# Two of every 125 row gathers of a graph kernel moved from GpSimd's indirect DMA to ScalarE, one transfer per row

## The reference

```python
def _L2_gnn_ref(feat, weight, src, dst, etypes):
    num_rels = weight.shape[0]                         # 16
    h_src = feat[src]
    msg = jnp.zeros((h_src.shape[0], weight.shape[2]), dtype=feat.dtype)
    for r in range(num_rels):
        mask = etypes == r
        msg = msg + h_src * mask[:, None].astype(feat.dtype) @ weight[r]
    return jax.ops.segment_sum(msg, dst, num_segments=feat.shape[0])

x = _layernorm(x + _L0_gnn_ref(...), axis=-1)
x = _layernorm(x + _L1_gnn_ref(...), axis=-1)
x = _layernorm(x + _L2_gnn_ref(x, L2_gnn_weight, src, dst, edge_type_16), axis=-1)
x = _layernorm(x + _L3_gnn_ref(...), axis=-1)
```

## Time and profile before

| | us |
|---|---|
| median of three runs | 13239.03 |
| the profiled execution's own time | 13241.2 |
| its span, first to last instruction | 13239.5 |
| POOL busy | 9829.3 (74%) |
| DVE busy | 6151.1 (46%) |
| PE busy | 2706.8 (20%) |
| ACT busy | 1294.2 (10%) |
| 3125 gathers of the relational layer: POOL busy, and idle just before them | 2965.0 and 1015.6 |
| the loop over these gathers | 4881.6 to 8801.9 |

### The profile page before, as it was taken

The page is one execution under the profiler, slowest core; times in us unless marked ns, Lnnn a source line. Parts: engine busy times, 40 slices in busy tenths (PEclk is TensorE's granted clock), DMA queues, the critical chain, the costliest instruction groups (busy, mean ns, idle before and its releaser), DMA issues. The chain is left out here.

```text
span 13239.5 us, 78693 instructions
## 1 busy us (share of the span) xinstructions
PE 2706.8 (20%) x12129; PEld 1928.6 (15%) x12156; DVE 6151.1 (46%) x21235; ACT 1294.2 (10%) x3683; POOL 9829.3 (74%) x10101
## 2 busy tenths in 40 slices
PE   2000001111100360000000000013444444444445
PEld 2000001111100230000000000002222322223232
DVE  8666547777753442222222222223555555555554
ACT  3011101111111230000000000000100001010101
POOL 7777757777777767777777777777777777777774
PEclk6555555555555675555555555555666666666665
DMA  6333334444444342222222222222222222222221
GB/s 168 101 101 102 102 98 118 118 118 118 117 118 117 115 144 63 67 63 67 67 63 67 63 67 63 67 54 51 65 65 67 66 66 65 65 65 65 66 66 32
DMA packets 731548, 1103.23 MB, mean 83 GB/s; under 512 B 240731, under 2 KB 347192, under 8 KB 730567
## 3 DMA queue, kind: packets, MB, share of 16 engines
q0 software_dynamic: 332944, 306.83, 12.5%
q1 hardware_dynamic: 231478, 567.25, 11.4%
q10 hardware_dynamic: 167040, 228.30, 5.7%
HBM read 548.64 MB, written 552.93 MB: 83 GB/s over the span
## 5 line engine op out<-in xcount | busy, mean ns | idle before, releaser
L130 POOL DMA_INDIRECT g<-in_edge_attr,idxs x3072 | 3119.5, 1015 | 1018.4 <-issue 856.8
L130 POOL DMA_INDIRECT msg<-Y,idx x3125 | 2965.0, 949 | 1015.6 <-issue 952.1
L130 POOL DMA_INDIRECT yg<-ytab,idx x3125 | 2949.8, 944 | 962.8 <-issue 950.2
L1420 DVE SCALAR_TENSOR_TENSOR run<-run,same,msg 128x64 f32<-128x64 f32 x3125 | 890.9, 285 | 3029.8 <-DMA msg<-Y,idx 2922.3
L485 DVE SCALAR_TENSOR_TENSOR run<-run,sameD 128x80 f32<-128x80 f32 x3072 | 911.6, 297 | 1578.3 <-DMA g<-in_edge_attr,idxs 1038.5
L1814 DVE SCALAR_TENSOR_TENSOR run<-run,same,ps 128x32 f32<-128x32 f32 x3125 | 775.0, 248 | 1636.0 <-PE ps L1708 1533.0
L1008 PE MATMUL ps<-tail,before 128*128 128x64 f32 (+2 forms) x10 | 2.8, 421 | 4575.7 <-PEq L1322 3930.5
L489 DVE SCALAR_TENSOR_TENSOR runS<-runS,sameS,g 128x64 f32<-128x64 f32 x3072 | 856.4, 279 | 0.3
L1797 DVE SCALAR_TENSOR_TENSOR zx<-zx,same,zs 128x32 f32<-128x32 f32 x3124 | 792.3, 254 | 136.5 <-DVE anew L1780 29.1
L1689 PE MATMUL ps<-eaT,W1e 128*128 128x512 f32 (+1 forms) x394 | 401.1, 1121 | 1972.2 <-DMA yg<-ytab,idx 1971.6
L1816 DVE SCALAR_TENSOR_TENSOR run<-run,anew,ps 128x32 f32<-128x32 f32 x3125 | 758.4, 243 | 0.0
(11 more groups left out here) (325 smaller groups left out, 6042.2 us busy)
## 6 DMA issues: line engine op xcount, KB each, us to landing
R<-run SPq DMA_DIRECT2D x390, 320.0 KB, 2.3
R<-run SPq DMA_DIRECT2D x195, 512.0 KB, 2.7
R<-run SPq DMA_DIRECT2D x124, 800.0 KB, 3.8
v<-in_edge_attr ACTq DMA_DIRECT2D x384, 256.0 KB
RA<-runS SPq DMA_DIRECT2D x256, 256.0 KB, 3.0
Y<-tab SPq DMA_DIRECT2D x98, 512.0 KB
msg<-Y,idx POOLq DMA_INDIRECT x3125, 2.4
Z<-zeros SPq DMA_DIRECT2D x125, 400.0 KB, 4.2
```

Source lines behind the costliest of these rows:

```text
L130: eng.indirect_dma_start(out=out, out_offset=None, in_=table, in_offset=bass.IndirectOffsetOnAxis(ap=index, axis=0)).then_inc(sem, 16)
L1420: ins_ = v.scalar_tensor_tensor(out=run[:, q, t, :], in0=prev, scalar=same[:, q, t:t + 1], in1=msg[:, q, t, :], op0=ALU.mult, op1=ALU.add)
```

## The change

One tile in slot 1 and one in slot 3 of each chunk, tile 12 of the 25 (`BY_ROW`, `ROW_AT`), is no longer fetched by POOL. ACT fetches it. For that, SP writes the row numbers of these tiles once to a DRAM table `rows2` [50, 128], ahead of the load of `x` in `edges_01`. In `edges_2` ACT, behind its two copies for slot 1 or 3, loads 16 row numbers at a time into registers and issues one DMA of one row for each: 8 register loads and 128 DMAs to a tile. They raise the new semaphore `by_row[q]`, for which DVE waits as well as for `got[q]`.

```diff
+BY_ROW, ROW_AT, ROW_REGS = (1, 3), 12, 16
 ...
             sp.wait_ge(x_clear, 1)
+            for h, q in enumerate(BY_ROW):
+                sp.dma_start(k.rows2[h * CHUNKS2:(h + 1) * CHUNKS2, :].rearrange("c p -> p c"),
+                             k.rel_i[:, :].rearrange("p (c t) -> p c t", t=CH2)[:, :, SL2 * q + ROW_AT],
+                             allow_slow_non_contiguous=True).then_inc(settled, 16)
             sp.dma_start(k.X[0:LASTP, :, :], ins["x"][0:LASTP * NB, :].rearrange("(p b) f -> p b f", b=NB)).then_inc(settled, 16)
 ...
-            sp.wait_ge(settled, 16 * (NW + 5 + 2 + 6))
+            sp.wait_ge(settled, 16 * (NW + 5 + 4 + 6))
 ...
+        by_row = {q: sem(f"msg_rows{q}") for q in BY_ROW}
 ...
                     act.copy(same[:, q], k.same[:, at]).then_inc(meta_ready, 1)
+                    if q in by_row:
+                        fetch_rows(c, q)
+
+            def fetch_rows(c, q):
+                at = BY_ROW.index(q) * CHUNKS2 + c
+                for a in range(0, P, ROW_REGS):
+                    _, rows = nc.values_load_multi_w_load_instructions(
+                        k.rows2[bass.ds(at, 1), a:a + ROW_REGS], engines=[act.engine], min_val=0, max_val=NP * RELS - 1,
+                        skip_runtime_bounds_check_because="a source node and a relation give a row of Y")
+                    for i, row in enumerate(rows):
+                        act.dma_start(msg[a + i:a + i + 1, q, ROW_AT, :], k.Y[bass.ds(row, 1), :]).then_inc(by_row[q], 16)
 ...
                 for t in range(SL2):
+                    if q in by_row and t == ROW_AT:
+                        continue
                     gather(pool, msg[:, q, t, :], k.Y, idx[:, q, t:t + 1],
 ...
-                            v.wait_ge(got[q], 16 * SL2 * (c + 1))
+                            v.wait_ge(got[q], 16 * (SL2 - (q in by_row)) * (c + 1))
+                            if q in by_row:
+                                v.wait_ge(by_row[q], 16 * P * (c + 1))
```

More of the change, by code:

```diff
@@ L2110, in build @@
         k.Y = dram("Y", [NP * RELS, D])
+        k.rows2 = dram("rows2", [CHUNKS2 * len(BY_ROW), P], I32)
         k.ytab, k.ztab, k.Z = dram("ytab", [NP, MSG]), dram("ztab", [NP, MSG]), dram("Z", [E + NP, MSG])
```

## The result

The changed kernel takes 13,425.6 us (median of 4 runs, 13,401 to 13,455), the kernel before 13,239.7 beside it: ratio 1.0141, interval 1.0115 to 1.0166, so +186 us where +661 was forecast. The profiled execution's own time is 13,454.9 with a span of 13,452.5, 213.0 us over the span of before.

The account below looks back on a forecast made before the run. POOL's gathers bound the loop before; ACT's stream, 129.3 + 51.2 + 2 = 182.5 us a chunk, would bound it after. The loop's +651.5 and the setup's 9 make +660.5, so 13,900 us, range 13,190 to 14,450.

Parts of the forecast that it names:

- What bounds the loop: In the loop: POOL's stream of gathers alone, 1.2536 us a tile; 50 gathers removed are worth 62.7 us.
- ACT becomes the bound, POOL waits for its `same` copy: In the loop: ACT needs 182.5 us a chunk against POOL's 154.2, so POOL waits 28 us at slots 2 and 4.
- A group of loads, 3.2 us: In ACT's stream: table address, then 16 row numbers, two memory trips of 1.6 us; 51.2 us a chunk.
- An issue, 0.505 us: In ACT's stream: one transfer with its register computation, 256 a chunk, 129.3 us.
- the lower bound of 0.435: In ACT's stream: lowest price in us of a one-row transfer, 0.27 for the issue plus 0.165 for the rest.
- the loop's +651.5: The loop's forecast growth in us, 4571.9 instead of 3920.4.
- The range: Whole kernel: 13,190 to 14,450 us; the main forecast's own part, 13,275 to 14,450, varies loads from 1.6 to 4.5 us a group.
- Rival 1: In the loop: ACT keeps up if a load group costs at most 1.43 us; time about 13,205 us; chance 0.29.
- The setup, 9 us forecast: Ahead of the load of x: writing 6400 single numbers delays POOL one for one, 5.2 to 21 us, taken as 9.
- the upper bound, 53 ns for each single number of 4 bytes: In the setup: price from 640 numbers landing after 3.7 us, 40 to an engine; gives 21 us in all.
- Rivals 2 and 3: Rival 2: one-row issues wait for landings, 20,900 us, chance 0.04; Rival 3: setup cost eats the gain, about 13,239 us, 0.05.
- Rival 3: In the setup: ACT keeps up, but 6400 single numbers cost 36 us or more; time near 13,239 us; chance 0.05.

Follow-up runs that it names:

- e15: The changed kernel with one register load of 16 row numbers a tile instead of eight, all 6400 one-row transfers kept, output partly wrong: 13,213.0 us, ratio 0.9976.
- e12: The changed kernel with 32 row numbers to a register load instead of 16: 13,214.1 us, 0.9986 of the kernel before.
- e14: The kernel before plus only the setup, two loads of row numbers ahead of x, no tile fetched by ACT: 13,265.9 us, ratio 1.0027.
- e16: The changed kernel with only one tile of 125 fetched by ACT, that of slot 3: 13,227.5 us, 0.9974 of the kernel before.
- e13: The kernel before, no tile by row, with the load of x cut into 112 and 15 partitions: 13,162.3 us, ratio 0.9941.
- e2: The changed kernel with the row numbers loaded behind x, on a slow chip where the kernel before takes 15,850 us: ratio 1.1663.
- e5: The changed kernel with the row numbers loaded behind x, on a slow chip where the kernel before takes 15,790 us: ratio 1.178.
- e11: The changed kernel with the row numbers loaded behind x instead of ahead of it: 13,376.8 us, 1.0101 of the kernel before.

## Why the forecast was right in kind and wrong in size

1. **What bounds the loop: right.** POOL's stream was all of it; e15, which takes 50 gathers away and adds no wait, has the loop 65 us shorter than before against 62.7 forecast.
2. **ACT becomes the bound, POOL waits for its `same` copy: right**, but at slot 4 alone, not at 2 and 4, outside chunk 0. ACT's wait for DVE is gone, as foretold, and nothing else is late for it: the loop ends 3.4 us after POOL's last gather, 3.3 before, and the program 4437 us after the loop in both.
3. **A group of loads, 3.2 us: right, in part by luck.** 3.34 measured. The picture was two trips of 1.6 us; it is 1.15 for the address and 1.95 for 16 numbers, two misses that go opposite ways, and that second part grows by 0.108 a register (e12). The Trainium skill, "Runtime: NRT & Kernel Launch", section Instruction fetch mechanics, gives about 200 ns a register; the 18 registers of a group here took 3.1 us, 172 ns each, but the added registers only 108.
4. **An issue, 0.505 us: the step that failed.** It is 0.414 in the mean, 0.380 in the median, under the lower bound of 0.435 too. I took the step from transfers of 128 rows, whose DMA instruction takes 0.35; for one row it takes 0.224, less than any short-row issue of SP that the trace showed. The rest of a step is what it was there, 0.51 - 0.35 = 0.16 against 0.380 - 0.224. 256 x 0.091 = 23.3 us a chunk, 25 times over, is 582 us of loop; loads, copies and the loop's end took 4.3 a chunk more than forecast, 108 us, and the difference, 474, answers to the 472 by which the loop's +651.5 was too much (+179.4). The range held the time all the same, but by its width in another term: it let the loads run from 1.6 to 4.5 us a group and kept the issue at 0.505.
5. **The sum with measured terms closes.** 182.5 - 23.3 + 16 x 0.14 for the loads + 2.1 for the copies and the loop's end = 163.5 us a chunk. Counted another way, a tile takes 79.8 us in the mean from its first load to its last issue, and 4.0 us of a chunk are left for the rest. In the trace chunk 0 ends its last wait 141.8 us after the first gather, and chunks 1 to 24 take 163.5 us each (162.5 to 166.5). 141.8 + 24 x 163.5 + 34.4 behind the last wait = 4100.2; measured 4099.8.
6. **Why the error counted so much.** POOL has 154.2 us a chunk of its own, so only what ACT needs beyond that is paid: 28 us forecast, 9 measured. An error of 12% in ACT's chunk made the loss three times too large. The point from which Rival 1 decides was worked out from the same dear issue: at 0.414 an issue and 4 us of copies, a group may cost (154.2 - 106 - 4) / 16 = 2.76 us, and the real one missed that by 0.6. e12 gets below it, by its 5.0 us for 32 numbers, and comes out near Rival 1's 13,205 (13,214). Its waits in chunk 0 sum to 15 us, between the 23 and the 5 that Rival 1 names, but at slots 2 and 4, where Rival 1 has slot 4 alone, and its setup is dearer.
7. **The setup, 9 us forecast, 21 at the upper bound: 20 to 23 on POOL's stall, +21 by e14's span.** The row I kept as the upper bound, 53 ns for each single number of 4 bytes, came out right in its sum; going by the stores of the earlier trace rows, 13 ns a piece of 128 bytes, misled. Why a piece of 4 bytes costs more than one of 128 is not shown; the records of the single numbers in the changed kernel's trace have a median of 9 ns and a mean of 46, so a minority of long ones makes the price. e16, with half of the numbers, has half of the price: 9.9 us.
8. **Rivals 2 and 3 fell.** The longest of 6400 issues took 1.01 us, under the 1.6 of a landing, and the median 0.224, so issues do not wait for landings. Rival 3 needs ACT to keep up and 36 us for the setup; ACT did not, and the setup took 20 to 23.

## What to carry to other kernels

When work moves to an engine that stands idle, what counts is that engine's stream against the period of the engine relieved: below it the move is worth its gain, less what the first round waits (15 us of 63 in e12, none in e16), and above it the stream's excess is paid every round (9 us, 25 times). Near that threshold a forecast needs the price of exactly the instruction to be issued, so where the trace has only larger ones, both bounds have to be stretched. Load row numbers with more registers at once (32 instead of 16 halved the address loads and ended POOL's waits behind chunk 0; more were not tried), and put nothing ahead of a transfer on which the other engines wait; a load of 127 partitions cut into 112 and 15 was worth 80 us, more than the idea that was to be tried.

## What the runs showed of the hardware that was not expected

- Loading registers from memory on ACT: 1.95 us for 16, 3.68 for 32, so 0.108 us for each one added; the load of the table's address ahead of it 1.15 us (medians of `after` and e12).
- A one-row transfer with its row in a register is issued every 0.38 us on ACT (median), every 0.31 without the address computation; 6400 of them lengthened POOL's gathers by no more than 2 ns (0.950 us in the mean in the changed kernel, 0.948 in e15 and 0.949 before).
- 3200 numbers of 4 bytes in DRAM held the queue behind them for about 10 us (e16; 20 to 23 for 6400), so 50 ns each, as an estimate, if they are spread over 16 engines, 200 to each.
- A load of 3.1 MB into 127 partitions moved its 127 pieces one after another, 0.95 us each, at 25 GB/s (before); into 112 and 15 partitions it was done in 17 us, with up to 17 pieces at once (e13).
- On two chips ACT's issues of one row came down to 3.5 to 4.9 us apart while POOL gathered, and the change with its row numbers behind x cost 17 and 18% (e2, e5) instead of 1.0% (e11).
